# Three loads of wqa instead of one, and three buffers of down-projection weights instead of five

## What is computed

```python
q = hidden_states @ wq_a.T                 # [.., 2048] @ [2048, 1536]
q = _rmsnorm(q, q_norm_w)
q = (q @ wq_b.T).reshape(b, s, NH, D_QK)
...                                        # attention, @ wo.T
x = _layernorm(x + attention(x))
gate = silu((x @ w_gate) * s_gate)         # 2048 -> 8192, int8 weights
up   = (x @ w_up) * s_up
y    = ((gate * up) @ w_down) * s_down     # 8192 -> 2048, int8 weights
x = _layernorm(x + y)
```

## Time and profile before

| | us |
|---|---|
| two runs of the kernel before | 8457.95 and 8581.43, median 8519.69 |
| the profiled execution | 8450.12, of which the slowest core's span is 8448.6 |
| spans of the 8 cores in it | 8403.7 to 8448.6 |
| PE busy | 7526.0 (89%) |
| DVE busy | 3988.1 (47%) |
| ACT busy | 3163.3 (37%) |
| POOL busy | 706.6 (8%) |

### The profile page before, as it was taken

One profiled execution on the slowest core, in us unless ns is written; L12 is line 12 of the kernel. 1 busy time (PEld: TensorE's weight loads), 2 busy tenths in 40 slices (PEclk: granted clock), 3 DMA queues, 4 the chain that ended last, 5 costly groups with the idle time before them and its releaser, 6 DMA issues. The chain is left out here.

```text
span 8448.6 us, 114847 instructions; the slowest of 8 cores (8403.7 to 8448.6 us)
## 1 busy us (share of the span) xinstructions
PE 7526.0 (89%) x37936; PEld 3010.9 (36%) x37936; DVE 3988.1 (47%) x4829; ACT 3163.3 (37%) x3449; POOL 706.6 (8%) x1160
## 2 busy tenths in 40 slices
PE   7877988899888899888999886989989989999997
PEld 3334632223232323232323221434434434444443
DVE  2123577788777787777777775511011011111101
ACT  2202555576565576565676554210000001000000
POOL 0000100000000000000000000011221231132122
PEclk8888999999999999999999997999999999999998
DMA  4224510000000000000000003454774584486457
GB/s 68 58 70 92 101 20 10 10 8 2 10 10 10 10 8 2 10 10 10 8 7 5 8 3 81 171 169 153 234 242 150 182 276 165 151 255 216 148 192 249
DMA packets 329898, 756.49 MB, mean 90 GB/s; under 512 B 88323, under 2 KB 90371, under 8 KB 321029
## 3 DMA queue, kind: packets, MB, share of 16 engines
q0 software_dynamic: 235840, 609.59, 24.7%
q1 hardware_dynamic: 93510, 139.56, 5.0%
HBM read 490.36 MB, written 62.91 MB: 65 GB/s over the span
## 5 line engine op out<-in xcount | busy, mean ns | idle before, releaser
L951 DVE TENSOR_TENSOR lac_sb<-lac_sb,at_sb 128x1024 f32<-128x1024 f32 x2016 | 2469.5, 1225 | 241.6 <-ACT at_sb L918 35.5
L918 ACT ACTIVATE at_sb<-scp,bias_sb 128x1024 bf16<-128x1024 f32 x2048 | 2274.2, 1113 | 460.6 <-PE scp L901 319.4
L933 PE MATMUL avp<-at_sb,V_sb 128*128 128x512 bf16 x4096 | 1257.1, 390 | 53.3 <-DVE aob L961 41.3
L887 PE MATMUL scp<-qfn,kf_sb 128*128 128x512 bf16 x4096 | 1256.3, 389 | 21.1 <-ACT at_sb L918 21.0
L1234 PE MATMUL e_g<-e_h1t,e_gw 128*128 128x512 bf16 x4096 | 939.1, 383 | 80.4 <-DVE e_fuse L1252 31.2
L1252 DVE SCALAR_TENSOR_TENSOR e_fuse<-e_u,su_sb,e_silu 128x512 bf16<-128x512 f32 x256 | 191.8, 750 | 1617.5 <-ACT e_silu L1247 1617.5
L1239 PE MATMUL e_u<-e_h1t,e_uw 128*128 128x512 bf16 x4096 | 925.8, 379 | 0.0
L1282 PE MATMUL e_d<-e_wd,e_fuse 128*128 128x512 bf16 x2048 | 797.6, 389 | 97.8 <-DVE e_ob L1308 68.3
L901 PE MATMUL scp<-qfp,k_pe 64*128 64x512 bf16 x2048 | 809.3, 395 | 0.0
L897 PE MATMUL scp<-qfp,k_pe 64*128 64x512 bf16 x2048 | 809.1, 395 | 0.0
L1286 PE MATMUL e_d<-e_wd,e_fuse 128*128 128x512 bf16 x2048 | 796.6, 389 | 0.0
(11 more groups left out here) (164 smaller groups left out, 5757.4 us busy)
## 6 DMA issues: line engine op xcount, KB each, us to landing
e_wd<-wd POOLq DMA_DIRECT2D x512, 512.0 KB, 3.7
e_gw<-wg POOLq DMA_DIRECT2D x256, 512.0 KB, 3.5
e_uw<-wu POOLq DMA_DIRECT2D x256, 512.0 KB, 4.2
xw<-x_full POOLq DMA_DIRECT2D x64, 512.0 KB, 5.4
d_xo<-x_own SPq DMA_DIRECT2D x16, 1024.0 KB, 8.6
h_sp<-d_h1b SPq DMA_DIRECT2D x16, 1024.0 KB, 3.8
e_h1r<-h_sp SPq DMA_DIRECT2D x16, 1024.0 KB, 10.6
out<-e_ob SPq DMA_DIRECT2D x16, 1024.0 KB, 6.5
```

The source lines that it names most:

```text
L887: t.matmul(scp[idx % 2][:, o:o + wd], kf[:, ks * P:(ks + 1) * P], qfn[hb][:, q0 + o:q0 + o + wd], start=True, stop=False)
L918: exd.inc(sc.activation(atb[:, idx % 4, 0:HF], scp[idx % 2][:, 0:HF], AF.Exp, bias=bias[:, 0:1], scale=SCALE))
L933: mm = t.matmul(avp[:, o:o + wd], Vt[:, ks, :], atb[:, idx % 4, o:o + wd], start=(ks == 0), stop=(ks == NKS - 1))
L951: ladc.inc(v.tensor_tensor(lac[:, qh % 2, 0:HF], lac[:, qh % 2, 0:HF], atb[:, idx % 4, 0:HF], ALU.add))
```

## The change

The single load of `wqa` becomes three, one for each segment of 512 columns, with a semaphore each. The wait for it ahead of the spreading of `q_norm_w` is taken out; instead PE waits, in token tile 0 alone, ahead of segment 0, 1 and 2 for one, two and three of the loads. In the feed-forward network `wdb` has 3 buffers instead of 5: load `gli` waits until group `gli - 3` is done.

```diff
-        g.dma_start(wqa[:], d_wqa.rearrange("a p b -> p a b")).then_inc(wlg.h, 16)
-        wlg.v += 16
+        wql = GDma(nc, "b_wql", 3)
+        for wsg in range(3):
+            wql.dma(g, wqa[:, :, wsg * 512:(wsg + 1) * 512],
+                    d_wqa[:, :, wsg * 512:(wsg + 1) * 512].rearrange(
+                        "a p b -> p a b"))
         s.dma_start(c_qnw[:], d_qnw).then_inc(wl.h, 16)
         wl.v += 16
         _w(t, wl, wl.v)
-        _w(t, wlg, wlg.v)
...
+                if i == 0:
+                    wql.wait(t, seg + 1)
...
-        wdb = [alloc(f"e_wd{i}", [P, 2, 1024], BF16) for i in range(5)]
+        wdb = [alloc(f"e_wd{i}", [P, 2, 1024], BF16) for i in range(3)]
...
-        wdl = GDma(nc, "e_wdl", 5)
+        wdl = GDma(nc, "e_wdl", 3)
...
-                        if gli >= 5:
-                            _w(g, dnm, gli - 4)
-                        wdl.dma(g, wdb[gli % 5][:],
+                        if gli >= 3:
+                            _w(g, dnm, gli - 2)
+                        wdl.dma(g, wdb[gli % 3][:],
...
-                                         wdb[gli % 5][:, ici, 0:512],
+                                         wdb[gli % 3][:, ici, 0:512],
...
-                                    wdb[gli % 5][:, ici, 512:1024],
+                                    wdb[gli % 3][:, ici, 512:1024],
```

## The result

The changed kernel is slower: the ratio of its time to that of the kernel before is 1.0227, with an interval of 1.0162 to 1.0291. The changed kernel took 8669.32 and 8674.19 us, against 8457.95 at the lowest before; the forecast was 8727, within 8585 to 8830.

The account below looks back on a forecast made before the run. PE was taken to bound the kernel, with only buffer depth keeping the `e_wd` supply ahead. Buffer loop 202, late landings 45, third sweep 32 and `wqa` -2 gave +277 us on 8450.12: 8727 us, range 8585 to 8830.

Parts of the forecast that it names:

- What bounds: Down-projection sweeps: PE busy with little idle time, `e_wd` transfers nearly without pause, only buffer depth keeping supply ahead of PE.
- The turn: Down projection, one buffer's loop: 6.44 us against 5.18 with three buffers, 12.6 us lost per sweep, 202 us in all.
- late landings: Down projection: late `e_wd` tiles that five buffers hid cost 2.8 us per sweep with three, 45 us in all.
- The third sweep: Down projection beside SP's stores and loads: late `e_wd` no longer covered, 15.3 us per token tile, 32 us net.
- What costs nothing: Feed-forward semaphore waits, POOL's issues and next `gw` and `uw` loads: nothing added; 10 us if the cover failed.
- wqa: Query projection start: PE's wait removed, but x lands behind `wqa`; -2 us, between -2.7 and +3.9.
- The sum: Whole kernel: 202 + 45 + 32 - 2 = +277 us on 8450.12, giving 8727 us, +3.3%.
- The signs: Profile after: first sweep 68 to 71 us, third 83 to 90, `e_wd` waits 250 to 330, first `wqa` matmul near 72.
- A: Down projection: buffer loop hides itself, landings at their shortest, late ones absorbed; +143 us, 8593 us; chance 0.13.
- B: Down projection: PE's clock falls after stops; 90 us more, 8820, or 9000 if all; chance 0.10 for 8820 or worse.
- C: Query projection: `wqa` pays more, PE starting some 28 us sooner were x not held behind it; 8700 us; chance 0.03.
- D: Down projection: the buffers do nothing since PE was never ahead; kernel gains 3 us, 8447; chance 0.02.

## Why the prediction was right, point by point

**What bounds.** Right: PE in the sweeps, with the supply one turn away from it. One reading on the way was wrong, and nothing rests on it: the idle time of the earlier trace rows is 8.6% of the busy time in line 1234 (80.4 of 939.1) and 12.3% in line 1282, not "over 2% against over 10%".

**The turn.** Right in mechanism and size: 6.44 us were predicted. Measured over all turns of core 0 after the change: 2.50 us from a group's start to the issue at the median, 3.68 to the landing, and 0.35 to PE in the chain above. The mean turn in ordinary sweeps is 6.69, which holds the late landings; 10 x (6.69 - 5.18) = 15.1 us per sweep. Predicted for turn and late landings together were 12.6 + 2.8 = 15.4, and the ordinary sweeps grew by 14.9 (56.8 to 71.7). The trace does not part the two terms cleanly, as a late landing now only lengthens a turn. The medians of the parts add up to 6.53 us, which over 160 turns is an estimated 216 us, and leaves some 22 of the 238 (16 x 14.9) for late landings. So the first term (202) was probably some 14 us too small and the second (45) some 23 too large; that their sum came out is in part luck. The landings did stay as they were, but not for the reason given: a load goes out 1.73 us after the one before and lands after 3.6, so two are under way at a time before the change, and the one is not over when the next is issued.

**The third sweep.** This term failed: 8 us for each token tile, 32 in all, where the third sweeps grew by 15.6 us (67.2 to 82.8) and the ordinary ones by 14.9, so 3 us in all. It was the difference of two numbers: 15.3 us that SP's traffic would cost a third sweep with three buffers, and 7.3 that it costs with five (a fourth of the 29.1 us of waits). The runs without that traffic measured 11.5 and 9.7, so both were off, one way each.

The 15.3 counted three late landings, with 4.4, 6.9 and 4.0 us of loss. In the chain after (start us, us, what) PE starts on the tiles of one buffer, three groups apart, at these times of the first token tile's third sweep:

```profile
6143.26 0.38 PE e_d L1286
...
6154.06 0.59 PE e_d L1286
...
6166.54 0.59 PE e_d L1286
...
6170.70 3.63 DMA e_wd<-wd
6174.33 0.24 issue
6174.57 0.38 PE e_d L1286
```

The turns are 10.8, 12.5 and 8.0 us, against 6.6 for an ordinary one: 4.2, 5.9 and 1.4 lost. The first two hold the late landings, and lose about what was forecast for them, though in the second PE ran for 5.7 us at the lower clock and that is part of it. The third has no late landing (3.63 us); what lengthens it are 8 matmuls at the lower clock behind the stop, one each 0.43 us instead of 0.216. A third stop by a late load, as I had counted it, did not come.

The 7.3 counted PE's waits alone. But behind the second and the third of the three waits PE ran for a while at the lower clock (for the second see the earlier trace rows), and that time is SP's too: PE was busy for 60.40 us of the third sweep in the earlier trace rows, and for 56.60 in the window without the traffic above.

Tile `e_wd` over the loads of the third sweep, before (25 loads) and after (26):

```profile
DMA to landing us min/median/max: 3.5/4.1/12.6
```

```profile
DMA to landing us min/median/max: 3.6/3.7/10.0
```

With more loads under way more of them are caught late: over the four third sweeps 11 to 13 of the 32 loads took over 4.5 us with five buffers, 7 or 8 with three.

**What costs nothing.** Right as far as it shows: the feed-forward stage of core 0 as a whole (first matmul of line 1234 to the end) grew by 236 us, less than its down projection, so nothing was lost in gate and up.

**wqa.** Predicted -2 within -2.7 to +3.9, measured -0.2. The first matmul that uses `wqa` starts at 73.79 instead of 73.97. The timeline after:

```profile
18.54 3.44 POOL L66 DMA_DIRECT2D wqa_sb<-wqa  x3 [16.29 <-POOLq L195]
...
66.26 1.86 PE L275 MATMUL trx_ps<-ident_bf,b_xw 128*128 128x128 bf16 x16 [38.31 <-DMA b_xw<-x_own]
...
73.79 12.19 PE L301 MATMUL ql_ps<-wqa_sb,b_xT 128*128 128x512 bf16 x48
```

The mechanism was right: PE's wait went over from `wqa` to x behind it on the queue (38.31 us). The loads of x lie 2.6 us further back in POOL's order, the last third of `wqa` lands at 20.8 + 42.6 = 63.4 instead of 61.0 (44.9 us from the first issue to the last landing, against 42.9 for the single load), and the two eat up the 2.7 us.

**The sum.** 8727 predicted, 8669 and 8674 measured, some 55 lower. Of that 37 are in the down projection (279 predicted, 242 measured), 29 of them the third-sweep term. The rest is in the base, not in the change. The profiled execution before had four cores, 0 among them, at a granted clock of 0.81 during the query projection, and four at 1.00; here core 0 and core 2 in the same stretch:

```profile
80.00:240.00 160.00, 160.00 (x833) 77.70 (x832) 51.68 (x43) 51.16 (x146) 5.29 (x10) 0.81 0.23 37
```

```profile
80.00:240.00 160.00, 159.26 (x999) 83.66 (x1012) 61.24 (x51) 62.30 (x176) 5.28 (x10) 1.00 0.22 37
```

It ended at 288.9 us on core 0 and at 260.2 on core 2, and core 2's span was 8403.7 us against 8448.6. Since core 0 after the change ended it at 262.0, its spans differ by only 209 us though the down projection grew by 242. The split of `wqa` does not do this: with the single load of before and three buffers core 0 ended it at 261.8 as well, and with the split cores 6 and 7 of the changed kernel still had 0.81. Why some cores get it and others not stays open. Against cores 2 to 5 of before (8403.7 to 8422.6) the change costs 230 to 250 us, 2.8%.

**The signs.** The first sweep took 71.4 us in the first token tile and 68.4 to 69.5 in the others, for the 68 to 71 forecast; POOL's issues come in threes (0.7 us each, 1.73 apart, then a pause); the landings stayed. The third sweeps are at 82 to 84 us, at the low end of 83 to 90. PE's waits were to be 250 to 330 us and the profile shows 218.0; with the 36 us that it leaves out they are 254. They are also not one before every third group but 220, against 160 turns: the loss of a turn is often spread over two groups. The first `wqa` matmul was to start near 72 and started at 73.79.

**The rivals.** A (the turn hides itself) fell with the landings, which stayed at 3.7. B fell for the stops of 1.3 us: 1.00 in the first sweep. Behind stops of 4 us its mechanism is there, as the third sweep shows. C and D fell too: x did hold PE back, and the buffers did what they should. What the chances for "slower" rested on was a margin of 277 against 169 us; at 242 it was nearer than I had it, and the interval of the ratio reaches down to 1.6%.

## What to carry to other kernels

A ring of buffers is hidden or not by one comparison: the turn (work on the buffer, release to issue, issue to landing, landing to the matmul) against the number of buffers times the work on one. All its parts can be read from a trace in which it is still hidden, and the loss has an edge there instead of a slope: here the step from five to four buffers cost 2 us per sweep, that from four to three 13. If memory is what is wanted, smaller tiles in more buffers shorten the turn at the same bytes; the time of one issue, 0.55 us here, is the next thing to compare, though no run reached it. And a load that is split so that work can start early gained nothing here as long as another operand of that work stood behind it in the same queue.

## What the runs showed of the hardware that I had not expected

- Beside SP's traffic the median landing of `e_wd` hardly depends on how many loads are under way (4.1 us with five buffers, 3.7 with three); the number of late ones and the longest do (12.6 us against 10.0).
- POOL issued one load of 256 KB written each 0.55 us where buffers stood free.
- Cores of one execution can differ in granted clock over a single stage: 0.81 on cores 0, 1, 6 and 7 and 1.00 on cores 2 to 5 in the query projection before, 28 us of difference at the end of that stage. Two profiles of one core can differ by that much with no change in the kernel.
- Each semaphore wait that PE still has to pass once the one that blocked it is met costs it some 0.1 us: from the landing to the next matmul it was 0.14, 0.24 or 0.35 us with three semaphores, 0.13 or 0.14 with one, and up to 0.66 with six.
